# Opening loads, row loads and modulation products of two softmax layers in a four-layer transformer kernel

## The reference

```python
mod = (_silu(L0_c) @ L0_wmod).reshape(L0_c.shape[0], 6, 1, -1)
sa, ca, ga, sb, cb, gb = (mod[:, 0], mod[:, 1], mod[:, 2], mod[:, 3], mod[:, 4], mod[:, 5])
ga = (2 * (ga >= 0) - 1) * jnp.maximum(jnp.abs(ga), 0.25)
gb = (2 * (gb >= 0) - 1) * jnp.maximum(jnp.abs(gb), 0.25)
h = _layernorm(x, axis=-1) * (1 + ca) + sa
x = x + ga * _L0_attn_ref(h, L0_attn_Wq, L0_attn_Wk, L0_attn_Wv, L0_attn_Wo, ...)
h = _layernorm(x, axis=-1) * (1 + cb) + sb
x = x + gb * _L0_ffn_ref(h, L0_ffn_W1, ...)
# the same for L1, L2 and L3, each with its own c and wmod
```

## Time and profile before

| what | us |
|---|---|
| three timed runs | 2247.33, 2253.03, 2253.18 (median 2253.03) |
| profiled execution | 2250.09 |
| its span in the trace | 2248.3 |
| layer 0's first maximum | 31.44 |
| layer 0's last unit, merge to last exponential | 642.66 to 670.83 |
| layer 1's first maximum | 754.53 |
| layer 1's last unit, merge to last exponential | 1068.98 to 1087.80 |

### The profile page before, as it was taken

One profiled execution on the slowest core, in us unless ns is written; L12 is line 12 of the kernel. 1 busy time (PEld: TensorE's weight loads), 2 busy tenths in 40 slices (PEclk: granted clock), 3 DMA queues, 4 the chain that ended last, 5 costly groups with the idle time before them and its releaser, 6 DMA issues. The chain is left out here.

```text
span 2248.3 us, 40661 instructions
## 1 busy us (share of the span) xinstructions
PE 2083.6 (93%) x15918; PEld 919.8 (41%) x15918; DVE 1581.1 (70%) x1988; ACT 1365.1 (61%) x2715; POOL 204.6 (9%) x382
## 2 busy tenths in 40 slices
PE   6999999999999699999889999999998989999998
PEld 2222222222234222222346566656665534444453
DVE  6999999999944899999445555555555265555553
ACT  4899999999974399999644444454445232222253
POOL 3011101110112311111000000000000010000000
PEclk7999999999989699999999999999999999999999
DMA  3010101010010101010100111011101124545420
GB/s 94 2 27 14 31 21 30 15 31 21 20 26 0 44 21 25 25 33 8 27 5 12 22 14 23 11 24 14 21 10 20 26 69 114 129 112 127 115 64 19
DMA packets 106861, 82.42 MB, mean 37 GB/s; under 512 B 54832, under 2 KB 89520, under 8 KB 102720
## 3 DMA queue, kind: packets, MB, share of 16 engines
q1 hardware_dynamic: 106016, 79.55, 15.5%
q0 software_dynamic: 480, 0.26, 0.1%
q10 hardware_dynamic: 192, 0.20, 0.0%
HBM read 62.98 MB, written 2.42 MB: 29 GB/s over the span
## 5 line engine op out<-in xcount | busy, mean ns | idle before, releaser
L1025 DVE TENSOR_REDUCE a0nm<-ps 128x2 f32<-128x1024 f32 x512 | 586.4, 1214 | 13.2 <-PE ps L892 11.1
L1003 ACT ACTIVATE a0p<-ps 128x512 f32<-128x512 f32 x1024 | 544.6, 599 | 74.9 <-PE ps L912 58.7
L926 PE MATMUL ps<-a0p,a0vst 128*32 128x256 f32 x4096 | 333.7, 397 | 26.9 <-ACT a0p L1003 13.9
L1025 DVE TENSOR_REDUCE a1nm<-ps 128x2 f32<-128x1024 f32 x256 | 294.5, 1215 | 10.4 <-PE ps L892 9.5
L1003 ACT ACTIVATE a1p<-ps 128x512 f32<-128x512 f32 x512 | 275.6, 596 | 40.5 <-PE ps L912 31.6
L912 PE MATMUL ps<-a0qm,a0k 32*128 32x512 bf16 x1024 | 278.1, 390 | 0.0
L1851 DVE TENSOR_REDUCE canm<-ps 128x1 f32<-128x128 f32 (+7 forms) x256 | 182.1, 753 | 115.3 <-PE ps L1714 114.5
L1802 ACT ACTIVATE cap_long<-ps,canm 128x1024 f32<-128x1024 f32 (+3 forms) x128 | 121.5, 952 | 190.1 <-DVE canm L1851 190.1
L2083 ACT ACTIVATE ex_s<-ps 128x512 f32<-128x512 f32 x128 | 76.4, 597 | 253.0 <-PE ps L2038 253.0
L892 PE MATMUL ps<-a0k,a0q 32*128 32x512 bf16 x1024 | 203.0, 395 | 23.4 <-DVE a0nm L1025 19.9
L926 PE MATMUL ps<-a1p,a1vst 128*32 128x256 f32 x2048 | 164.1, 392 | 6.4 <-ACT a1p L1003 5.5
(11 more groups left out here) (316 smaller groups left out, 2497.2 us busy)
## 6 DMA issues: line engine op xcount, KB each, us to landing
ex_wb<-ex_w_dram SPq DMA_DIRECT2D x62, 512.0 KB, 6.1
carrow<-car_dram SPq DMA_DIRECT2D x32, 256.0 KB, 4.3
xc_res<-a0rec SPq DMA_DIRECT2D x15, 256.0 KB
a0q<-a0parts_sb SPq DMA_DIRECT2D x96, 32.0 KB, 2.0
a0k<-a0parts_sb SPq DMA_DIRECT2D x96, 32.0 KB, 2.0
a1q<-a1parts_sb SPq DMA_DIRECT2D x96, 32.0 KB
...
```

The source lines that it names most:

```text
L926: last = pe.matmul(R.ps[32 * j:32 * j + 32, 6, cols], vst[:, g, s, j * HG // 4, :], p[:, s % 2, j, cols], start=(g == 0 and s == 0 and hal ...
L1003: act.activation(p[:, s % 2, e, :], R.ps[:, score_bank(n), :], ACT.Exp).then_inc(exp_done, 1)
L1025: dve.tensor_reduce(nm[:, u % 2, tb, 2 - 2 * z:4 - 2 * z, hf], R.ps[:, bank:bank + 2, :], X_AXIS, ALU.max, negate=True).then_inc(bank_free, 1)
```

## The change

1. *Opening loads.* The first chunk of `x` is loaded by ACT, the second by SP behind the identity, then cT, layer 0's modulation weights, layer 0's query and key weights, the second batch's row and the value weights. TensorE makes six products of `ones` with `ones` into an unused bank before the first centring product.
2. *Norm of three chunks first.* `Norm` takes `chunks`; in layer 0 the norm of chunk 3 is cut off. Its centring product stands behind the first projections, its square behind ACT's splits, its variance product behind the values, its logarithm and exponential behind ACT's loads, its VectorE steps last before the first maxima. Chunk 3's values stand behind slots 2 and 3, its queries and keys in halves of 256 columns behind slots 4 to 7 (in both layers). Values use banks 0, 1, 6, 7, the second batch's queries and keys banks 4 and 5; remainders lie in `xc` instead of `sq`. The waits for values before slots 0 and 1 become `A.cleared`; `v_done[1]` and the modulation's copy are waited for behind the first maxima.
3. *Row loads on three queues.* In layer 0 too GpSimd issues key part 0; ACT issues key parts 1 and 2 and, in both layers, query part 2; SP query parts 0 and 1 and the mask.
4. *Modulations one layer ahead.* Three parts: layer 0, layer 1, layers 2 and 3. Layer 1's six products stand behind slots 8 to 13 of layer 0's first maxima; the twelve of layers 2 and 3 behind slots 0 to 3 and 8 to 15 of layer 1's. ACT copies them, VectorE's six steps stand at the start of the maps' combination and of layer 1's output. The last unit holds none.

```diff
-    PARTS = (slice(0, 1), slice(1, LAYERS))
+    PARTS = (slice(0, 1), slice(1, 2), slice(2, LAYERS))
...
+    def copy_act(act):
+        act.wait_ge(products, turn + 1)
+        act.activation(mod, made, ACT.Copy).then_inc(step, 1)
...
-    loads = [(S.ident_loaded, R.ident[:], dram["ident"]), (S.x_loaded[0], R.x[:, 0], dram["xT"][:, 0]), (M.cT_loaded, M.cT[:], dram["cT"]),
-             (M.loaded[0], M.w[:, 0, :], dram["L0_wmod"]), (S.x_loaded[1], R.x[:, 1], dram["xT"][:, 1])]
+    loads = [(S.ident_loaded, R.ident[:], dram["ident"]), (S.x_loaded[1], R.x[:, 0, CW:T], dram["xT"][:, 0, CW:T]),
+             (M.cT_loaded, M.cT[:], dram["cT"]), (M.loaded[0], M.w[:, 0, :], dram["L0_wmod"])]
+    loads += [(W.front_loaded, dst, src) for dst, src in W.front[:2]]
+    loads += [(S.x_loaded[2], R.x[:, 1], dram["xT"][:, 1])]
+    loads += [(W.front_loaded, dst, src) for dst, src in W.front[2:]]
...
     def on_act(act):
+        act.dma_start(R.x[:, 0, 0:CW], dram["xT"][:, 0, 0:CW]).then_inc(S.x_loaded[0], 16)
...
     def on_pe(pe):
+        pe.wait_ge(R.setup_sems.ones_done, 3)
+        for i in range(6):
+            pe.matmul(R.ps[:, 7, 0:C], R.ones[:], R.ones[:], start=True, stop=True)
+        pe.wait_ge(R.setup_sems.centre_done, 1)
         norm.centre(pe, 0)
         norm.centre(pe, 1)
-        pe.wait_ge(R.setup_sems.ones_done, 3)
         norm.variance(pe, 0)
         products(pe)
         norm.centre(pe, 2)
         norm.variance(pe, 1)
         norm.variance(pe, 2)
-        pe.wait_ge(step, 1)
-        norm.centre(pe, 3)
-        norm.variance(pe, 3)
+        pe.wait_ge(*steps[0])
...
+    VALUES = (0, 1, 6, 7)
+    A.cleared = [(v_done[0], 8), (S.logged, n0 + NC) if last_chunk else (rested, 4)]
...
-        for part in range(3):
-            for o in range(2):
-                if bias and o == 1:
-                    continue
-                part_waits(sp, part, o)
-                load_rows(A, 0, 0, o, sp, (part,))
...
+        for part in range(2):
+            part_waits(sp, part, 0)
+            load_rows(A, 0, 0, 0, sp, (part,))
...
         first_batch(0)
         first_batch(1)
+        if last_chunk:
+            last_chunk.centre(pe, 3)
         second_batch(2, 0)
         second_batch(2, 1)
-        for c in range(NC):
-            values(c)
-        A.among_maxima = {1: lambda: second_batch(3, 0), 3: lambda: second_batch(3, 1)}
+        values(0)
+        values(1)
+        values(2)
+        A.among_maxima = {4: lambda: second_batch(3, 0, range(0, 1)), 5: lambda: second_batch(3, 0, range(1, 2)),
+                          6: lambda: second_batch(3, 1, range(0, 1)), 7: lambda: second_batch(3, 1, range(1, 2))}
+        slots = [*range(8, 14)] if last_chunk else [*range(4), *range(8, 16)]
...
+        if last_chunk:
+            pe.wait_ge(rested, 4)
+            last_chunk.variance(pe, 3)
+            A.among_maxima.update({2: lambda: values(3, range(0, 2)), 3: lambda: values(3, range(2, 4))})
+        else:
+            values(3)
...
+        if last_chunk:
+            last_chunk.square(act, 3)
+        act.wait_ge(A.inited[0], A.n_inited[0])
+        for part in (1, 2):
+            part_waits(act, part, 1)
+            load_rows(A, 0, 0, 1, act, (part,))
+        load_rows(A, 0, 0, 0, act, (2,))
+        if last_chunk:
+            last_chunk.invert(act, 3)
         for c in (2, 3):
+            for o in range(2):
+                first_part(2 * c + o)
             if not bias:
                 copy_values(c)
-            for o in range(2):
-                first_part(2 * c + o)
...
         pe.wait_ge(*A.projected)
+        pe.wait_ge(A.v_done[1], 8)
+        pe.wait_ge(*A.modulation[3][0])
...
-                if A.modulation and u == UNITS - 1 and 0 < s < 7:
-                    A.modulation[0](pe, s - 1, 6)
...
         if A.maps:
+            A.modulation[2](dve)
             lambda_programs(W)[2](dve)
             for c, rows in COMBINED:
-                if c == 3:
-                    A.modulation[1](dve)
```

176 lines of the change are left out of this document (96 added, 80 removed).

## The result

The changed kernel takes 2235.97 us (median of four executions, 2235.10 to 2236.80) against 2252.07 for the kernel before, run beside it (four, 2247.33 to 2253.18). The ratio on record is 0.9937, with a 95% interval of 0.9923 to 0.9952 (the two medians divided give 0.9929, inside it). The forecast was 2233 with a range of 2226 to 2242. The profiled execution has a span of 2235.0, 13.3 less than the 2248.3 of before, where the sum of the forecast had 18.4.

What follows compares the result with a forecast made beforehand. VectorE's row maxima were taken to bound the softmax layers, leaving gains only at their ends. 12.5 + 5.1 - 0.3 + 1.1 = 18.4 off 2250.09 gives 2231.7, partly taken back to 2233 us; range 2226 to 2242.

Steps and rivals of the forecast that it cites:

- Modulations out of the last unit: Layer 0's end: without modulation products the last unit is as long as layer 1's, at full clock; gain about 12.5.
- the 657 of the forecast: Layer 0's last unit: GpSimd's squares of the last maps estimated done near 657, four before the head sums at 660.9.
- The bounds of 9.4 and 13.5: Layer 0's end: gain of 9.4 if only the unit's length counts, 13.5 with TensorE's part wholly halved from 672.11 on.
- The opening: Before layer 0's first maximum: three-chunk norm and new load order bring it to 26.3 against 31.44; gain about 5.1.
- Their use can only be the clock: Opening: six products of ones on idle TensorE can only help by raising the clock; part of 2.2 gained in the norm.
- bounds of 3.3 and 5.92: Opening: landing time of x's first chunk, 3.3 if its 256 KB came first, 5.92 if bytes ahead count; 5.2 taken.
- Among layer 0's first maxima: Layer 0's sixteen first maxima: inserted products overrun their slots, 1.4 lost instead of 1.1; a loss of 0.3.
- Overrun 6 x 0.42, less 0.5 that the two bank pairs absorb: Layer 0's first maxima at low clock: inserted work overruns slots, 2.0 lost instead of 1.1; at full clock all fits.
- rival 1: Both layers' first maxima: clock stays at 1.2 GHz and late second parts delay the first turn; costs 5, time 2238; chance 0.14.
- Layer 1: Before layer 1's first maximum: query part 2 leaves SP, first scores 1.3 earlier, inserted products cost 0.2; gain about 1.1.
- everything behind layer 1 as before: Steady units and everything after layer 1 were expected unchanged.

Runs made afterwards that it cites:

- Experiment 1: Changed kernel with all 18 modulation products of layers 1 to 3 back in layer 0's last unit, in six shares of three: 2248.29 us, ratio 0.9997.
- the second trace of before: Kernel before the change, run again unaltered for a second profiled execution: median 2248.27 us, ratio 0.9996; the profiled execution took 2247.39.
- experiment 5: Changed kernel without the six products of ones at the start: 2235.73 us, ratio 0.9938.
- Experiment 8: Changed kernel with the work among layer 0's first maxima cut finer and spread by what a slot holds at the low clock: 2235.29 us, ratio 0.9928.

## Why the prediction was right, and where not

**Modulations out of the last unit (12.5).** Measured 12.74 against the profiled execution, by the reason given: TensorE reached the head sums 18.33 after the merge (forecast 18.20), without a wait for the squares, at full clock, and the logarithm came 12.74 earlier once the gain that arrived with the unit is taken off (16.17 less 3.43). Experiment 1 gives 12.3 in the times. The clock is 8.1 of the 12.74 (6.5 in the unit, 1.6 behind it). The last squares were done at 651.64, well before the 657 of the forecast. What the forecast did not see is that this price belongs to an execution: against the second trace of before it is 8.96, of which the clock is 4.2, and that lies under the lower bound. The bounds of 9.4 and 13.5 were set by sizes of work, and not by when the clock falls. That the term came out within 0.3 is in part luck: it was taken from the same execution of before that it is measured against.

**The opening (5.1).** Measured 5.36, and the bound moved from the loads to chunk 3's norm, as forecast; the first remainder (16.04 for 15.9) and the last split (21.29 for 21.2) hit. Its first step was wrong all the same. "Their use can only be the clock" was worked out as a good part of 2.2, and experiment 5 finds 0.3. In the changed kernel the centring was not on the path: the chunk landed at 4.32, where I took 5.2 between bounds of 3.3 and 5.92, and then the table load at 6.06 to 7.34 was last. By the rows the step that gave the time is the small first load, behind which even the slow centring of experiment 5 ends at 8.01, where before it ended at 9.67. That is argued: no run puts the row back into one load.

**Among layer 0's first maxima (-0.3).** Measured -1.95. The step that failed is "Overrun 6 x 0.42, less 0.5 that the two bank pairs absorb", with 1.4 taken between full and low clock. The clock was at 0.50 for all of it; a half projection kept TensorE 1.15 (31.28 to 32.44) and not 0.95, with its scores 1.69 a slot where a maximum needs 1.14 to 1.23. Five slots at 1.69 instead of 1.13 make 2.8 of the 3.1 that the phase has over 18.3. Experiment 8 takes 1.7 of it away. This was the first half of rival 1, its clock; the second half (a turn that waits for GpSimd) did not happen in the changed kernel and did in experiment 8.

**Layer 1 (1.1).** The first scores came at 739.17 instead of 753.87, 14.70 earlier, of which 13.23 had arrived with the norm: 1.47 for 1.3. Its maxima lost 0.64 and 0.35 against the first trace of before but 0.06 and 0.04 against the second. So the term is 0.5 to 1.4.

**Outside the sum.** The forecast held "everything behind layer 1 as before" and spoke of nothing between the layers. There the profiled executions differ by 2.9 in a stretch whose program is unchanged, and the lengths of the product groups in it give the same 2.9 (4.4 of low clock less 1.5). Terms forecast: 18.4. Terms measured in the two first traces, without that stretch: 5.36 - 1.95 + 12.74 + 1.47 - 0.64 - 0.35 = 16.6. Medians: 16.1. The forecast of 2233 was 3 too low, by the first-maxima term (1.65 worse than forecast), by layer 1's maxima and by sizing all against one execution; how the 3 divide among these is not shown.
